# Four-layer gated cross-attention stack: where the FFN weights are loaded, and how the second attention opens

## The chip, the cores and the metric

One core of a Trainium2 chip runs the whole program in one launch. The metric is the device time of that core in microseconds (us). The engines are TensorE (PE, with its weight loads as PEld), VectorE (DVE), ScalarE (ACT), GpSimd (POOL) and SyncE (SP); SP issues nearly all transfers of this kernel, a few come from ACT's queue.

## The reference

Sixteen batches of 256 tokens with 256 features pass four residual layers. The context has 77 rows per batch.

```python
x = x + tanh(g_xattn[0]) * attention_16_heads_of_16(layernorm(x), ctx)     # q, k, v, out with biases
x = x + tanh(g_ffn[0])   * quantised_ffn(layernorm(x))                     # 768 hidden, 4-bit weights in blocks of 32
x = x + tanh(g_xattn[1]) * attention_8_heads_of_64(layernorm(x), ctx)
x = x + tanh(g_ffn[1])   * butterfly_ffn(layernorm(x))                     # W_exp, 10 stages, gelu, 10 stages, W_con

# attention:      softmax(q k^T / sqrt(d)) v, then the output projection
# quantised_ffn:  act_qdq around every product; weights wq = clip(round(w / s)) * s, s = max|w| / 7 per block
# butterfly:      per stage, pairs (i, i + 2^stage) are mixed by 2 x 2 matrices
```

## The kernel before

**Arithmetic.** Every fp32 product is done as three passes of rounded halves (`three_passes`, L41 to L43: hi x hi, hi x lo, lo x hi). x stays in SBUF as `xres` over the whole program. The butterfly stages are multiplied out on the chip to two matrices, w1 (tile `f_y`) and w2 (`f_z`), beside the quantised FFN; both are stored to DRAM (`w_spill`) and loaded back for the last layer.

**First attention** (`stacked_attention`). It runs in slots, one for each batch b, and each engine has its own written order of steps for a slot: `PE_SLOT`, `DVE_SLOT` and so on, SP's at L658. In a slot the engine works on several batches: the load of x (`xl`) and its layer norm (`ln`) are for batch b+4, the queries for b+3, the stacked keys and queries for b+2 (`qw`, `qr`, `k0`, `k1`), the maxima of the scores (`mx0` to `mx7`) for b+1, and the output with its update of x (`pu`) for b-1. SP's steps are `xl` (L149, x of b+4), `qw` (L327, stores the queries to DRAM), `vb` (L772), `k0` and `k1` (L318, keys), `qr` (L336 and L338, loads the queries back as a stack), and at b = 0 and b = 1 `save`: the values of the second attention are stored to DRAM (L287), since the tile that holds them, `a_keys_then_fw`, is to take the raw FFN weights. At b = 1 SP then waits until these stores are read (L292) and loads the three weight matrices (`load_ffn`, 768 KB each). A slot is called by its b below. Its DVE order begins with maxima `mx0` to `mx3`, then `ln`, then `mx4` to `mx7` and `pu` (L924). From slot 3 on (`FW_FIRST`) a few quantising steps `w0` to `w5` (L65 to L75) stand between them in each slot; they all wait for one semaphore that counts the three loads.

**The quantised FFN's last block and the passage.** The last block of `quantised_ffn` computes the down projection and, on the side, the last butterfly product, whose two additions POOL does (L2325). SP issues what the second attention needs first: weights `wq` and `wo`, the saved values (L2357), the first keys (L2365), a picking mask (L2368), and then the store of w1 (L2370). At its end SP waits for both stores (L2371, L2372), as they sit in tiles that the next block reuses. A block of the program ends with a barrier over all engines (L48, L49).

**Second attention** (`late_attention`). Again slots by batch, with the orders that `slots` takes. Its first slots are partial: slot -2 and -1 prepare batches 0 and 1. Batch 0's queries come from the block before, in banks `T0` and `X0`. Per batch: ACT rounds the queries to `q_hi` (L1354); DVE splits off the remainder (L1508); the upper halves are copied by DMA to two tiles (L1363 for batch 0, on ACT's queue; L1246 later); SP loads the keys `kb` (L1265) and `kz` (L1259); PE multiplies q_hi by `kz` into the bank `T0` in four groups and DVE reduces each to maxima (`mx0` to `mx3`, L1614 and L1515); PE transposes the maxima (`mt`, L1620), ACT spreads them over rows of `a_q_max` (L1374), and the scores (`s0` to `s3`, L1639 and L1641) take them as part of the contraction. `kb` also holds, in part 1 of its middle index, the picking mask, which ACT writes for the two first buffers (`pick`, L1319) before the keys may be loaded over its rows (L1265). POOL clears `a_q_max` (L1280) and `kz[1]` (L1281) at the start. At batch 0's `mt` ACT also computes the gate's tanh (L1368) and, one instruction later, the first exp (L1369), which brings in that function's table.

## Time and profile before

| | |
|---|---|
| Time, three runs | 1073.12 us median (1069.98, 1073.12, 1073.65) |
| The profiled execution | 1070.05 us, of it 1068.3 us span |
| PE, PEld busy | 927.3 us (87%), 821.2 us (77%) |
| DVE busy | 769.8 us (72%) |
| ACT, POOL busy | 604.2 us (57%), 283.2 us (27%) |
| Mean granted clock of PE | 0.938 of full |

Start times in the rows are us from the span's start. In a row of the timeline the bracket says how long the engine had been idle and what released it. "SPq" and "ACTq" are DMA issues on these engines' queues. Slot 1 of the first attention runs at about 76 to 88 us, slot 2 at 88 to 112, slot 3 at 113 to 125, and the passage into the second attention lies between 600 and 660 us. A granted clock of 1.00 is TensorE at 2.4 GHz, 0.50 is 1.2 GHz.

### The profile page before, as it was taken

To read this page: it belongs to the slowest core of one execution; us is meant where nothing else is said; L and a number is where in the kernel's file an instruction comes from. 1 tells how busy PE (TensorE), PEld (TensorE's weight loads), DVE (VectorE), ACT (ScalarE), POOL (GpSimd) and SP (SyncE) were. 2 spreads that over 40 slices of the span, in tenths; PEclk is the share of its full clock that TensorE was granted. 3 is DMA by queue.
4 is the path that set the end of the run, shared out by engine and by line. 5 is a ranking of instruction groups with operands and counts; after the bars stand their busy time and mean duration, and the time that the engine had idled before them with its cause. 6 is when DMAs were issued, how large, how long until landed. Compare 5 with 4: busy or idle time off the path is not lost. (4 is left out here: it accounts for less than half of the span.)

```text
span 1068.3 us, 19975 instructions
## 1 busy us (share of the span) xinstructions
PE 927.3 (87%) x6641; PEld 821.2 (77%) x6641; DVE 769.8 (72%) x1556; ACT 604.2 (57%) x1048; POOL 283.2 (27%) x480
## 2 busy tenths in 40 slices
PE   5896989999969999960369858999999979999998
PEld 5775877877767887750259857999999968988898
DVE  5534878887656888998987835777777869667671
ACT  4354666776646758879958625665666544222230
POOL 5302333330118914430014221111111123111210
PEclk9998999999988999985579987999999999999999
DMA  7657555565064317878801066655555510001001
GB/s 211 176 158 228 131 149 143 148 199 157 10 250 176 156 42 226 257 260 276 281 40 40 25 180 149 127 126 126 126 126 121 110 40 1 21 22 39 20 20 40
DMA packets 100137, 137.01 MB, mean 128 GB/s; under 512 B 42710, under 2 KB 75734, under 8 KB 97382
## 3 DMA queue, kind: packets, MB, share of 16 engines
q1 hardware_dynamic: 99158, 133.87, 44.2%
q10 hardware_dynamic: 608, 1.18, 0.4%
q0 software_dynamic: 304, 1.10, 0.3%
q8 instruction: 38, 0.62, 0.3%
q14 instruction: 29, 0.24, 0.1%
HBM read 68.47 MB, written 45.82 MB: 107 GB/s over the span
## 5 line engine op out<-in xcount | busy, mean ns | idle before, releaser
L2762 ACT ACTIVATE f_h<-bank,f_b 128x512 f32<-128x512 f32 x64 | 43.4, 690 | 112.3 <-PE bank L43 64.5
L912 DVE TENSOR_REDUCE a_maxima<-bank 128x4 f32<-128x308 f32 x128 | 60.4, 472 | 45.1 <-PE bank L1000 44.1
L41 PE MATMUL bank<-f_xt_hi,f_w_all 128*128 128x512 f32 x192 | 78.0, 406 | 6.8 <-DMA f_xt_lo<-x_spill 4.8
L835 ACT ACTIVATE a_prob<-bank 77x512 f32<-77x512 f32 x128 | 72.4, 588 | 18.5 <-PE bank L1025 18.2
L43 PE MATMUL bank<-f_xt_hi,f_w_all 128*128 128x512 f32 x192 | 76.6, 399 | 0.0
L42 PE MATMUL bank<-f_xt_lo,f_w_all 128*128 128x512 f32 x192 | 76.6, 399 | 0.0
L43 PE MATMUL bank<-f_w_hi,f_h_lo 128*128 128x256 f32 x256 | 72.4, 283 | 0.0
L42 PE MATMUL bank<-f_w_lo,f_h_hi 128*128 128x256 f32 x256 | 72.3, 282 | 0.0
L41 PE MATMUL bank<-f_w_hi,f_h_hi 128*128 128x256 f32 x256 | 72.0, 281 | 0.0
L1022 PE MATMUL bank<-a_stack,a_kb 96*77 96x256 f32 x256 | 70.9, 301 | 0.5 <-ACT a_mt L828 0.5
L1927 DVE TENSOR_REDUCE f_gmax<-f_hid 128x1 f32<-128x1024 f32 x48 | 55.6, 1213 | 15.4 <-ACT f_hid L2053 15.4
L1656 PE MATMUL bank<-a_values,a_prob 77*128 (+1 forms) x512 | 66.5, 273 | 0.0
L1025 PE MATMUL bank<-a_mt,a_pick 128*77 128x256 f32 x256 | 66.4, 283 | 0.0
L1000 PE MATMUL bank<-a_kb,a_stack 96*128 96x156 f32 x256 | 50.9, 281 | 17.6 <-DVE a_maxima L912 9.9
L1656 PEld LDWEIGHTS bank<-a_values,a_prob 77*128 77x128 f32 x512 | 62.2, 192 | 0.0
L41 PE MATMUL bank<-f_d_hi,f_w_all 128*128 128x256 f32 (+2 forms) x174 | 52.6, 302 | 7.6 <-DVE xres L2399 3.9
L1000 PEld LDWEIGHTS bank<-a_kb,a_stack 96*128 96x128 f32 x256 | 40.3, 194 | 23.4 <-DVE a_maxima L912 12.4
L41 PE MATMUL bank<-a_wo_hi,a_at_hi 128*128 128x256 f32 x192 | 57.6, 300 | 0.0
L43 PE MATMUL bank<-a_wo_hi,a_at_lo 128*128 128x256 f32 x192 | 54.4, 284 | 0.0
L42 PE MATMUL bank<-a_wo_lo,a_at_hi 128*128 128x256 f32 x192 | 54.4, 284 | 0.0
L1022 PEld LDWEIGHTS bank<-a_stack,a_kb 96*77 96x77 f32 x256 | 37.7, 147 | 21.1 <-issue 8.6
L41 PE MATMUL bank<-f_xt_hi,f_w_hi 128*128 128x512 f32 x128 | 51.8, 405 | 1.3 <-ACT f_h L2762 1.3
(332 smaller groups left out, 3181.2 us busy)
## 6 DMA issues: line engine op xcount, KB each, us to landing
u_spill<-f_ubuf SPq DMA_DIRECT2D x48, 256.0 KB, 2.4
f_w_all<-u_spill SPq DMA_DIRECT2D x24, 512.0 KB, 5.2
a_stack<-a_queries SPq DMA_DIRECT2D x16, 512.0 KB, 5.0
a_q_max<-a_q_hi SPq DMA_DIRECT2D x30, 256.0 KB, 4.5
a_kb<-a_key_spill SPq DMA_DIRECT2D x96, 77.0 KB, 2.6
xres<-in_x SPq DMA_DIRECT2D x16, 256.0 KB, 4.8
a_queries<-a_q_hi SPq DMA_DIRECT2D x16, 256.0 KB, 3.6
a_queries<-a_q_lo SPq DMA_DIRECT2D x16, 256.0 KB, 4.5
```

The costliest lines, as they stand in the source:

```text
L41: nc.tensor.matmul(out, w_hi, m_hi, start=start, stop=False)
L42: nc.tensor.matmul(out, w_hi, m_lo, start=False, stop=False)
L43: return nc.tensor.matmul(out, w_lo, m_hi, start=False, stop=stop)
L835: act.activation(prob[0:S, n % 4, :, :].rearrange("p a b -> p (a b)"), (S0, S1)[n % 2][0:S, :], ACT.Exp, scale=SCALE).then_inc(probs, 1)
L912: dve.tensor_reduce(maxima[:, t, 4 * k:4 * k + 4], MX[:, 0:4 * SE].rearrange("p (h s) -> p h s", s=SE)[:, :, 0:S], AX.X, ALU.max).then_inc ...
L1000: last = pe.matmul(MX[:, 2 * n * SE:2 * (n + 1) * SE], stack[0:ROWS, par, pair, t * P:(t + 1) * P], kb[0:ROWS, par, :, pair, :], start=Tru ...
L1022: pe.matmul(out, kb[0:ROWS, par, a, pair, 0:S], stack[0:ROWS, par, pair, :], start=True, stop=False)
L1025: last = pe.matmul(out, pick[:, 2 * pair + a, 0:S], mt[:, par, :], start=False, stop=True)
L1656: last = pe.matmul(out_of(t, h), prob[0:S, n % 2, a, t * P:(t + 1) * P], v, start=True, stop=True)
L1927: dve.tensor_reduce(gmax[:, side, m // 2:m // 2 + 1], hid[:, 2 * g:2 * g + 2, f - 1:f + 1, :], AX.XYZ, op).then_inc(g_maxed, 1)
L2762: act.activation(h[:, n % 2, :], hbank[n % 4][:, :], ACT.Gelu, bias=b1[:, n:n + 1]).then_inc(h_ready, 1)
```

## The change

There are two independent parts. In the first attention SP gets a step `fw` of its own at the end of slot 2 (b = `FW_FIRST - 1`), behind that slot's `k1`; the wait for the value stores and the loads of the FFN weights move there from the end of slot 1. The semaphore `fw_in` becomes three, one for each matrix (in `load_ffn` each load counts its own), and the quantising step of the first slot waits for the gate matrix alone; later ones wait for all three.

In the passage: the store of w1 stands behind the first keys' load, ahead of the mask and the values. DVE writes the picking mask (`pick0`, `pick1`) in an order `DVE_FIRST` that slot -1 alone uses, and there the four maxima come before the split of the queries. Batch 0's scores for the maxima go to four banks (S0, S1, O0, O1), need only the rounded queries, and its transposed maxima go to T1, so PE need not wait for DVE between groups. The keys of part 0 are loaded before part 1, and only part 1 waits for the mask. The gate's tanh and the exp that brings its table are done in the quantised FFN's blocks, the loads of the gate leave the passage and that of `bo` goes to SP behind batch 1's keys. POOL clears `a_q_max` for batch 0 only at the start and the rest after batch 1's layer norm, for which SP gets one more wait at batch 1.

```diff
@@ -655,7 +656,7 @@
-        SP_SLOT = "xl qw vb k0 qr k1 save keep".split()
+        SP_SLOT = "xl qw vb k0 qr k1 save fw keep".split()
@@ -663,7 +664,7 @@
-        ONLY_AT = {"save": (0, 1), "keep": (B - 6, B - 5, B - 4), "rk": (B - 3,), "sk": (B - 3,)}
+        ONLY_AT = {"save": (0, 1), "fw": (FW_FIRST - 1,), "keep": (B - 6, B - 5, B - 4), "rk": (B - 3,), "sk": (B - 3,)}
@@ -734,9 +735,9 @@
                         save_value(sp, i)
-                    if b == 1:
-                        sp.wait_ge(v1_saved, 16 * NV1)
-                        load_ffn(sp)
+                elif what == "fw":
+                    sp.wait_ge(v1_saved, 16 * NV1)
+                    load_ffn(sp)
@@ -901,7 +902,11 @@
                 elif what[0] == "w":
-                    dve.wait_ge(fw_in, 48)
+                    if isinstance(b, int) and b == FW_FIRST:
+                        dve.wait_ge(fw_in[0], 16)
+                    else:
+                        for loaded in fw_in:
+                            dve.wait_ge(loaded, 16)
@@ -1190,17 +1194,28 @@
+        DVE_FIRST = "pick0 ln mx0 mx1 mx2 mx3 q0 q1 pick1 xt".split()
...
-        def slots(eng, order, step, prepare=()):
+        def max_bank(b, g):
+            return (S0, S1, O0, O1)[g] if isinstance(b, int) and b == 0 else T0
+        def spread_bank(b):
+            return T1 if isinstance(b, int) and b == 0 else T0
+        def slots(eng, order, step, prepare=(), opening=None):
...
-                for what in order:
-                    if what in PRE:
+                for what in (opening or order) if isinstance(b, int) and b == -1 else order:
+                    if what[:4] == "pick":
+                        step(what, b, par)
+                    elif what in PRE:
@@ -1241,6 +1256,8 @@
                     sp.sem_inc(sp_passed, 1)
+                    if isinstance(b, int) and b == 1:
+                        sp.wait_ge(mt_cleared, 2 * HPC)
@@ -1258,12 +1275,16 @@
                                      late["k_dram"][own[a], 0, :, bass.ds(b * S, S)]).then_inc(kz_in[par], 16)
-                    if isinstance(b, int) and b < 2:
-                        sp.wait_ge(picked, b + 1)
-                    for a in range(HPC):
-                        for part, rows in ((0, own[a]), (0, across[a]), (1, own[a])):
-                            sp.dma_start(kb[rows, par, a, part, :, :].bitcast(F32),
-                                         late["k_dram"][own[a], part, :, bass.ds(b * S, S)]).then_inc(keys_in[par], 16)
+                    for part in range(2):
+                        if part and isinstance(b, int) and b < 2:
+                            sp.wait_ge(picked, b + 1)
+                        for a in range(HPC):
+                            for rows in (own[a], across[a])[0:2 - part]:
+                                sp.dma_start(kb[rows, par, a, part, :, :].bitcast(F32),
+                                             late["k_dram"][own[a], part, :, bass.ds(b * S, S)],
+                                             ).then_inc(keys_in[par], 16)
+                    if isinstance(b, int) and b == 1:
+                        sp.dma_start(bo_raw[:], gbias).then_inc(small_in, 16)
@@ -1276,12 +1297,11 @@
-            for a in range(HPC):
-                pool.memset(q_max[a][:].bitcast(F32), 0.0).then_inc(mt_cleared, 1)
-            pool.memset(kz[1][:].bitcast(F32), 0.0).then_inc(kb_cleared, 1)
...
+            def clear_max(par):
+                for a in range(HPC):
+                    pool.memset(q_max[a][:, par, :, :].bitcast(F32), 0.0).then_inc(mt_cleared, 1)
+            clear_max(0)
@@ -1297,6 +1317,12 @@
                     pool.tensor_tensor(nmr[:], nmean[:], rstd[:], ALU.mult).then_inc(ln_nmr, 1)
+                    if isinstance(b, int) and b == 1:
+                        pool.memset(kz[1][:].bitcast(F32), 0.0).then_inc(kb_cleared, 1)
+                        clear_max(1)
@@ -1315,16 +1341,9 @@
         def _(act):
-            def pick(n):
-                act.activation(kb[:, n, :, 1, :, :], late["pick_raw"][:, :, :, 0:S], ACT.Copy).then_inc(picked, 1)
...
                     if isinstance(b, int) and b == 0:
-                        act.dma_start(gate_raw[:], gate).then_inc(small_in, 16)
-                        act.dma_start(bo_raw[:], gbias).then_inc(small_in, 16)
-                        act.wait_ge(late["pick_in"], 16)
-                        pick(0)
@@ -1354,7 +1373,6 @@
-                        pick(1)
@@ -1363,16 +1381,14 @@
-                    if isinstance(b, int) and b == 0:
-                        act.wait_ge(small_in, 32)
-                        act.activation(tg[:], gate_raw[:], ACT.Tanh).then_inc(g_done, 1)
-                        act.activation(warm[:], gate_raw[:], ACT.Exp)
-                        act.wait_ge(mt_cleared, HPC)
+                    if isinstance(b, int) and b < 2:
+                        act.wait_ge(mt_cleared, (b + 1) * HPC)
...
-                                                  T0[0:HEADS, 0:T].unsqueeze(1).to_broadcast([HEADS, c1 - c0, T]),
+                                                  spread_bank(b)[0:HEADS, 0:T].unsqueeze(1).to_broadcast(
+                                                      [HEADS, c1 - c0, T]),
@@ -1437,6 +1453,10 @@
                     return
+                elif what[:4] == "pick":
+                    n = int(what[4])
+                    dve.wait_ge(late["pick_in"], 16)
+                    dve.tensor_copy(kb[:, n, :, 1, :, :], late["pick_raw"][:, :, :, 0:S]).then_inc(picked, 1)
@@ -1452,7 +1472,7 @@
-                        dve.wait_ge(g_done, 1)
+                        dve.wait_ge(small_in, 16)
@@ -1512,7 +1532,8 @@
-                    dve.tensor_reduce(maxima[:, t, h0:h0 + 4], T0[:, 0:4 * S].rearrange("p (h s) -> p h s", s=S),
+                    dve.tensor_reduce(maxima[:, t, h0:h0 + 4],
+                                      max_bank(b, g)[:, 0:4 * S].rearrange("p (h s) -> p h s", s=S),
@@ -1604,20 +1626,23 @@
-                        pe.wait_ge(q_split, b * NP + 1)
+                        if isinstance(b, int) and b == 0:
+                            pe.wait_ge(q_rounded, 1)
+                        else:
+                            pe.wait_ge(q_split, b * NP + 1)
...
-                    if not (isinstance(b, int) and b == 0 and g == 0):
+                    if not (isinstance(b, int) and b == 0):
...
-                        last = pe.matmul(T0[:, at:at + HPC * S], q_hi[:, n, t * P:(t + 1) * P],
+                        last = pe.matmul(max_bank(b, g)[:, at:at + HPC * S], q_hi[:, n, t * P:(t + 1) * P],
...
-                        last = pe.transpose(T0[0:HEADS, t * P:(t + 1) * P], maxima[:, t, :], ident[:])
+                        last = pe.transpose(spread_bank(b)[0:HEADS, t * P:(t + 1) * P], maxima[:, t, :], ident[:])
@@ -2231,6 +2257,7 @@
                 act.activation(tg[:], tg[:], ACT.Tanh)
+                act.activation(env["first"].tg[:], env["first"].tg[:], ACT.Tanh)
@@ -2351,12 +2378,6 @@
                 weight("wo")
-                wait_coded(sp, late["values_free"])
-                for half in range(2):
-                    bs = slice(half * B // 2, (half + 1) * B // 2)
-                    sp.dma_start(late["values"][0:S, bs, :, :].rearrange("p b h v -> p b (h v)"),
-                                 late["v_dram"][bs.start * S:bs.stop * S, :].rearrange("(b s) n -> s b n", s=S),
-                                 ).then_inc(late["values_in"][half], 16)
@@ -2364,10 +2385,16 @@
                                  late["k_dram"][half, 0, :, 0:S]).then_inc(first.kz_in[0], 16)
+                sp.wait_ge(y_add, 2 * TOP)
+                sp.dma_start(bf["w1_dram"], y[:]).then_inc(y_stored, 16)
...
                 sp.dma_start(late["pick_raw"], late["picks"]).then_inc(late["pick_in"], 16)
-                sp.wait_ge(y_add, 2 * TOP)
-                sp.dma_start(bf["w1_dram"], y[:]).then_inc(y_stored, 16)
+                wait_coded(sp, late["values_free"])
+                for half in range(2):
+                    bs = slice(half * B // 2, (half + 1) * B // 2)
+                    sp.dma_start(late["values"][0:S, bs, :, :].rearrange("p b h v -> p b (h v)"),
+                                 late["v_dram"][bs.start * S:bs.stop * S, :].rearrange("(b s) n -> s b n", s=S),
+                                 ).then_inc(late["values_in"][half], 16)
@@ -2497,6 +2524,7 @@
+                act.activation(warm[:], tg[:], ACT.Exp)
```

SP's order in the first attention around slots 1 to 3; `a_value_spill` is the value store, `a_keys_then_fw<-in_w_...` are the weights, `xres<-in_x` is x of b+4. Before:

```order
L287 DMA a_value_spill<-a_keys_then_fw 128x520 x4
L287 DMA a_value_spill<-a_raw 80x520
L292 DMA a_keys_then_fw<-in_w_gate 128x6x256
L292 DMA a_keys_then_fw<-in_w_up 128x6x256
L294 DMA a_keys_then_fw<-in_w_down 128x2x768
L149 DMA xres<-in_x 128x2x256
L327 DMA a_queries<-a_q_hi 128x512
L327 DMA a_queries<-a_q_lo 128x512
L772 DMA a_vb<-a_values 77x512
L318 DMA a_kb<-a_keys 16x624 x3
L336 DMA a_stack<-a_queries 64x2048
L338 DMA a_stack<-a_queries 32x2048
L318 DMA a_kb<-a_keys 16x624 x3
L149 DMA xres<-in_x 128x2x256
```

After:

```order
L288 DMA a_value_spill<-a_keys_then_fw 128x520 x4
L288 DMA a_value_spill<-a_raw 80x520
L149 DMA xres<-in_x 128x2x256
L328 DMA a_queries<-a_q_hi 128x512
L328 DMA a_queries<-a_q_lo 128x512
L773 DMA a_vb<-a_values 77x512
L319 DMA a_kb<-a_keys 16x624 x3
L337 DMA a_stack<-a_queries 64x2048
L339 DMA a_stack<-a_queries 32x2048
L319 DMA a_kb<-a_keys 16x624 x3
L293 DMA a_keys_then_fw<-in_w_gate 128x6x256
L293 DMA a_keys_then_fw<-in_w_up 128x6x256
L295 DMA a_keys_then_fw<-in_w_down 128x2x768
L149 DMA xres<-in_x 128x2x256
```

The three weight loads stood ahead of slot 2's x, queries, keys and stack; they now stand behind them and ahead of slot 3's x.

SP's order in the last block of the quantised FFN (`w_spill<-f_y` is the store of w1, `a_rest<-in_picks` the mask). Before:

```order
L2351 DMA w_spill<-f_z 128x2048
L2348 DMA a_raw<-in_wqkv 128x2x512
L2348 DMA a_raw<-in_wo 128x4x256
L2357 DMA a_values<-a_value_spill 77x8x520 x2
L2365 DMA a_kz<-a_key_spill 64x4x77 x2
L2368 DMA a_rest<-in_picks 128x624
L2370 DMA w_spill<-f_y 128x2056
```

After:

```order
L2378 DMA w_spill<-f_z 128x2048
L2375 DMA a_raw<-in_wqkv 128x2x512
L2375 DMA a_raw<-in_wo 128x4x256
L2386 DMA a_kz<-a_key_spill 64x4x77 x2
L2389 DMA w_spill<-f_y 128x2056
L2391 DMA a_rest<-in_picks 128x624
L2395 DMA a_values<-a_value_spill 77x8x520 x2
```

The store of w1 moved ahead of the mask and of the saved values.

DVE's order in the opening of the second attention, from the start of its block (`a_maxima<-bank` are the maxima, `f_xt_hi` and `f_xt_lo` the split of the queries, `a_kb<-a_rest` the mask). Before:

```order
L1444 BN_STATS a_bn<-xres 128x6 x2
L1452 BN_AGGR a_mv<-a_bn 128x2 x2
L1508 TENSOR_TENSOR f_xt_hi<-bank,a_q_hi 64x512
L1508 TENSOR_TENSOR f_xt_lo<-bank,a_q_hi 64x512
L1515 TENSOR_REDUCE a_maxima<-bank 128x4
L1508 TENSOR_TENSOR f_xt_hi<-bank,a_q_hi 64x512
L1508 TENSOR_TENSOR f_xt_lo<-bank,a_q_hi 64x512
L1515 TENSOR_REDUCE a_maxima<-bank 128x4 x3
L1499 TENSOR_TENSOR a_xt_lo<-bank,a_xt_hi 128x512
```

After:

```order
L1459 CAST a_kb<-a_rest 128x2x308
L1464 BN_STATS a_bn<-xres 128x6 x2
L1472 BN_AGGR a_mv<-a_bn 128x2 x2
L1535 TENSOR_REDUCE a_maxima<-bank 128x4 x4
L1528 TENSOR_TENSOR f_xt_hi<-bank,a_q_hi 64x512
L1528 TENSOR_TENSOR f_xt_lo<-bank,a_q_hi 64x512
L1528 TENSOR_TENSOR f_xt_hi<-bank,a_q_hi 64x512
L1528 TENSOR_TENSOR f_xt_lo<-bank,a_q_hi 64x512
L1459 CAST a_kb<-a_rest 128x2x308
L1519 TENSOR_TENSOR a_xt_lo<-bank,a_xt_hi 128x512
```

The four maxima stand together ahead of the split, and DVE has the two mask copies that were ACT's.

## Rows read from the trace of the kernel before

**Rows 1.** Timeline of SP's DMA issues: start, length, queue, line, transfer, count.

```profile
86.22 0.55 SPq L287 DMA_DIRECT2D a_value_spill<-a_raw  x1
92.41 0.38 SPq L292 DMA_DIRECT2D a_keys_then_fw<-in_w_gate  x1
...
94.01 0.75 SPq L149 DMA_DIRECT2D xres<-in_x  x1
...
103.61 0.49 SPq L336 DMA_DIRECT2D a_stack<-a_queries  x1
...
104.83 1.27 SPq L318 DMA_DIRECT2D a_kb<-a_keys  x3
```

**Rows 2.** Timeline of DVE, slots 2 and 3.

```profile
102.05 0.75 DVE L176 BATCH_NORM_STATS2 a_bn<-xres 128x6 f32<-128x256 f32 x2 [8.68 <-DMA xres<-in_x]
...
103.14 0.45 DVE L912 TENSOR_REDUCE a_maxima<-bank 128x4 f32<-128x308 f32 x1
...
110.70 0.88 DVE L924 SCALAR_TENSOR_TENSOR xres<-bank,a_tg,xres 128x256 f32<-128x256 f32 x2 [1.02 <-PE bank L43]
...
118.08 0.73 DVE L176 BATCH_NORM_STATS2 a_bn<-xres 128x6 f32<-128x256 f32 x2
...
119.16 0.45 DVE L912 TENSOR_REDUCE a_maxima<-bank 128x4 f32<-128x308 f32 x1
...
123.86 0.88 DVE L924 SCALAR_TENSOR_TENSOR xres<-bank,a_tg,xres 128x256 f32<-128x256 f32 x2 [0.17 <-PE bank L43]
```

**Rows 3.** Windows: length, busy us of PE, PEld, DVE, ACT, POOL, clock, DMA share, GB/s.

```profile
96.00:100.00 4.00, 0.00 (x0) 0.00 (x0) 0.00 (x0) 0.00 (x0) 0.00 (x0) 0.98 1.06 387
...
104.00:108.00 4.00, 4.00 (x24) 3.05 (x23) 2.15 (x4) 1.90 (x5) 0.61 (x2) 0.50 0.82 178
```

**Rows 4.** DMA issues, 85 to 125 us: count, KB each, median us to landing.

```profile
a_stack<-a_queries SPq DMA_DIRECT2D x2, 256.0 KB, 5.7
```

**Rows 5.** Waits of PE, 112 to 290 us: total, times, longest.

```profile
PE bank L1000 <- DVE a_maxima L912: 1.1, 2, 0.6
```

**Rows 6.** Waits of SP, 575 to 665 us: total, times, longest.

```profile
SPq L2372 <- DMA w_spill<-f_y: 11.4, 1, 11.4
```

**Rows 7.** Timeline of SP, 596 to 662 us.

```profile
615.96 3.60 SPq L2370 DMA_DIRECT2D w_spill<-f_y  x1
634.25 5.08 SPq L1265 DMA_DIRECT2D a_kb<-a_key_spill  x6
```

**Rows 8.** DMA issues, 596 to 650 us: KB, us to landing.

```profile
w_spill<-f_y SPq DMA_DIRECT2D x1, 1028.0 KB, 15.0
```

**Rows 9.** Timeline of POOL, same stretch.

```profile
597.97 5.06 POOL L2325 TENSOR_TENSOR f_y<-f_y,f_y_pair 128x1028 f32<-128x1028 f32 x2 [8.41 <-ACT f_y L2477]
...
632.59 3.54 POOL L1280 MEMSET a_q_max<- 128x2048 f32 x2 [17.69 <-POOLq L49]
```

**Rows 10.** Timeline of PE, same stretch.

```profile
627.27 0.28 PE L43 MATMUL bank<-a_rows_hi,a_wq_lo 128*128 128x256 f32 x1
636.28 0.68 PE L1614 MATMUL bank<-a_kz,a_q_hi 128*128 128x154 f32 x2 [8.73 <-DVE f_xt_lo L1508]
...
643.87 0.47 PE L1639 MATMUL bank<-f_xt_hi,a_kb 128*77 128x256 f32 x1 [0.41 <-DMA a_kb<-a_key_spill]
...
645.88 0.41 PE L1641 MATMUL bank<-a_q_max,a_kb 128*77 128x256 f32 x1
646.36 0.58 PE L41 MATMUL bank<-a_xt_hi,a_wq_hi 128*128 128x256 f32 x1
```

**Rows 11.** Timeline of ACT, same stretch.

```profile
635.23 0.53 ACTq L1363 DMA_DIRECT2D f_xt_hi<-a_q_hi  x1
...
639.66 1.28 ACT L1369 ACT_TABLE_LOAD   x1
...
642.72 2.39 ACT L1374 ACTIVATE a_q_max<-bank 8x256 fp32r<-8x256 f32 x4 [1.56 <-PE bank L1620]
```

**Rows 12.** Source line L2719, all its 64 casts: shortest, median, longest in ns.

```profile
L2719 DVE CAST f_h_hi<-f_h x64: 411/422/961, 881.3 to 1041.3; 128x512 fp32r<-128x512 f32 x64
```

**Rows 13.** Timeline of DVE and of POOL, 896 to 903 us.

```profile
898.74 0.96 DVE L2719 CAST f_h_hi<-f_h 128x512 fp32r<-128x512 f32 x1
...
897.54 3.90 POOL L2738 TENSOR_TENSOR xres<-xres,f_gb 128x256 f32 x4 [1.63 <-DVE f_xn L2709]
```

More of the change, by code:

```diff
@@ L220, in stacked_attention @@
         q_moved, kb_moved, vb_moved = ([sem(f"{x}{par}") for par in range(2)] for x in ("q_moved", "kb_moved", "vb_moved"))
-        sp_passed, scores, fw_in = sem("sp_passed"), sem("scores"), sem("fw_in")
+        sp_passed, scores = sem("sp_passed"), sem("scores")
+        fw_in = [sem(f"fw_in{n}") for n in range(3)]
         q_stored = [sem("q_stored0"), sem("q_stored1")]
@@ L1106, in late_tensors, with late_attention @@
     late["pick_raw"] = late["rest"][:, 0:heads * (S + S % 2)].rearrange("p (a c s) -> p a c s", c=C, s=S + S % 2)
-def late_attention(nc, env, gbias, gate):
+def late_attention(nc, env, gbias):
     HEADS, d = 8, 64
@@ L1155, in late_attention @@
         gb = sb("gb", [P, D])
-        tg = sb("tg", [P, 1])
+        tg = first.tg
         warm = sb("warm", [P, 1])
         bo_raw = sb("bo_raw", [P, D])
-        gate_raw = sb("gate_raw", [P, 1])
         xn = nxt.xn[:, 1, 0:TT, :]
@@ L1179, in late_attention @@
         passed, sp_passed, small_in = sem("passed"), sem("sp_passed"), sem("small_in")
-        next_cleared, mt_cleared, picked, g_done, gb_ready, biased = (sem(x) for x in (
-            "next_cleared", "mt_cleared", "picked", "g_done", "gb_ready", "biased"))
+        next_cleared, mt_cleared, picked, gb_ready, biased = (sem(x) for x in (
+            "next_cleared", "mt_cleared", "picked", "gb_ready", "biased"))
         q_rounded, q_split = sem("q_rounded"), sem("q_split")
@@ L1403, in step @@
                     act.activation(nxt.w2_hi[:], nxt.v, ACT.Copy).then_inc(nxt.v_rounded, 1)
-                    act.activation(warm[:], gate_raw[:], ACT.Gelu)
+                    act.activation(warm[:], tg[:], ACT.Gelu)
                 elif what in ("at0", "at1"):
@@ L1535, in _ @@
                    (B - 1, "q0"): "turn0", (B - 1, "q1"): "turn1", (B - 1, "mx1"): "next_xn1",
-                   (B - 1, "mx2"): "turn2", (B - 1, "at1"): "turn3", (B - 1, "mx3"): "next_x", (B, "norm"): "next_w2"})
+                   (B - 1, "mx2"): "turn2", (B - 1, "at1"): "turn3", (B - 1, "mx3"): "next_x", (B, "norm"): "next_w2"},
+                  DVE_FIRST)
         @block.tensor
@@ L2104, in _ @@
                 sp.dma_start(tg[:], gate).then_inc(g_in, 16)
+                sp.dma_start(env["first"].tg[:], late["gate"]).then_inc(g_in, 16)
                 sp.dma_start(paths, bf["low_paths"]).then_inc(paths_in, 16)
@@ L2570, in sem @@
             return self.sems[-1]
+        self.tg = sb("gate", [P, 1])
         self.minus_half, self.eps, self.zero = sb("minus_half", [P, TT]), sb("eps", [P, TT]), sb("zero", [P, TT])
@@ L2841, in build @@
         env["keys_dram"] = nc.dram_tensor("a0_keys", (2, B, P, DC, S + S % 2), F32, kind="Internal").ap()
-        env["late"] = late = {"ctx_t": a["ctx_t"], "wqkv": a["wqkv1"], "wo": a["wo1"], "picks": a["picks1"],
+        env["late"] = late = {"ctx_t": a["ctx_t"], "wqkv": a["wqkv1"], "wo": a["wo1"], "picks": a["picks1"], "gate": a["gx1"],
                               "inner": 512, "heads": 8}
@@ L2859, in build @@
                                   a["out_bias"], a["gf1"])
-            late_attention(nc, env, a["bo1"], a["gx1"])
+            late_attention(nc, env, a["bo1"])
             free_semaphores(nc, env["late"]["sems"] + env["first"].sems)
```

12 lines of the change are left out of this document (6 added, 6 removed).

## The prediction

> **What bounds the kernel now.** The page first: PE is busy 87% of the span, so a stretch in which PE stands still, or runs at the lower clock, is the place to look. The timeline of DVE shows the first one. In slot 2 DVE waits 8.68 us before the layer norm, and the releaser is the load of x [rows 2]. The maxima `mx4` to `mx7` stand behind that norm in DVE's order and PE has no free bank without them: from 96 to 100 us all engines are at zero while the DMA engines run at 387 GB/s, and afterwards PE works at clock 0.50 [rows 3]. SP's timeline says why x is late. The last value store is issued at 86.22, then SP waits until 92.41 for these stores, issues the three weight loads, and only at 94.01 the load of x [rows 1]. So x is issued some 7.2 us later than SP was free, and behind 2.3 MB.
>
> The second place is the passage. The wait list of SP has 11.4 us for the store of w1 at the block's end [rows 6]. That store is issued at 615.96 [rows 7] and lands 15.0 us later, at 630.96 [rows 8]; what it stores was ready at 597.97 + 5.06 = 603.03 [rows 9], and PE was done at 627.55 [rows 10]. The next block's first work starts at 632.59 [rows 9], 1.63 after the landing. I call this start T0. From there PE's first full stretch begins with the queries of batch 1 (`q0`) at 646.36, T0 + 13.77 [rows 10].
>
> **Part 1, the weight loads behind slot 2.** Removed: the 8.68 us. With SP free at 86.8, x for slot 2 is issued there and has only the value stores beside it; they are read by 92.4, when SP's wait for them ends [rows 1], and `ln` is reached at 102.05 - 8.68 = 93.4 [rows 2]. So x comes in time by about 1 us. Also removed: the slow clock behind the stall. From `mx4` to the update of x slot 2 needs 110.70 - 103.14 = 7.56 us, slot 3 the same work in 123.86 - 119.16 = 4.70 [rows 2]; 2.86 us more at the lower clock. Together 11.54.
>
> Given back in slot 3: its x now stands behind the weights. Slot 2's stack is issued at 103.61 before, when PE restarts, so now near 94.9; its `k1` follows and ends 2.49 us later [rows 1], at 97.4, and the weights follow. Slot 3's norm is reached at 118.08 before [rows 2], now at 106.5. When is x there? Lower bound: all that is issued from 94.9 on is 768 KB of stack, 117 KB of keys, 2304 KB of weights and 256 KB of x, 3.5 MB, at 387 GB/s [rows 3] 9.1 us, so 104.0: no wait. Upper bound: before, 102.05 - 92.41 = 9.64 us passed from the first weight load to x [rows 1, 2]; with the stack's own 5.7 us [rows 4] still wholly ahead, 97.4 + 9.64 + 5.7 = 112.7, a wait of 6.2. Without the stack's share it is 107.0, a wait of 0.5. The stack has half of its time behind it at 97.4, and the rate above is one with nothing small in it, so I take 107.7, a wait of **1.2** us. The first quantising step needs only the gate matrix now, the first of the three, so it doesn't add to this. The new waits for two more semaphores in each later step are on DVE, for which PE waits 1.1 us in twice from 112 to 290 us [rows 5]: nothing, at most 1. Part 1 gives 11.54 - 1.2 = **10.3** us (5.3 at the upper bound, and less if the clock falls again: 2.5).
>
> On this the Trainium skill (*DMA: Bandwidth & Descriptors*, section "Queues, rings and completion order") says that each DMA engine takes the descriptors of a queue's ring in ring order. The trace agrees: x issued at 94.01 came only at 102.05. By that rule x of slot 3 can't overtake the weights, and the saving is that of my sum as long as the weights are through before the norm; by it, the wait moves rather than goes if they aren't, the first rival below.
>
> **Part 2, the passage.** (a) The store of w1 is issued at about 603 to 606 now and, with 15.0 us at most, is down by 621, before PE ends at 627.55. What ends the block is then PE. With the same 1.63 us to the next block's first work the start is 629.2, T0' = T0 - **3.4**. The values and the mask stand behind the store; the values are not issued before 609.97 either way, since SP waited there for their tile, and PE needs them only in slot 0.
>
> (b) Within the passage two chains run to the first scores `s0`: the maxima and the DMAs. The chain of maxima is `mx0` at 636.28, T0 + 3.7, behind DVE's split [rows 10], four rounds of matmul and reduce, `mt`, and ACT's spreading at 642.72 to 645.11, T0 + 10.1 to 12.5 [rows 11]. In it go the three round trips, the split and the 1.28 us table load [rows 11]. With four banks the products follow ACT's rounding directly: from the rounding's end near T0' + 1.6, four pairs of 0.7 [rows 10], reduce and transposes about 1, the spreading 2.4 [rows 11], so done at about T0' + 8. The other chain: `s0` at 643.87 waited last for the keys [rows 10], first issued at 634.25 [rows 7], 9.62 us before. They were issued at T0 + 1.66, since ACT had to write the mask first; now part 0 is issued at T0' + 0.1. Then `s0` can start at T0' + 9.7 rather than T0 + 11.28, 1.6 us earlier. From `s0` to the end of `s1` are 646.29 - 643.87 = 2.4 us, in which 0.18 was a wait for ACT, so `q0` at T0' + 12.0 against T0 + 13.77 [rows 10]: **1.8** us. The DMA chain sets this, so the shorter maxima gain nothing beyond it. If the transfers land sooner, since 1.4 us less is queued and the upper halves are issued earlier than at 635.23 [rows 11], the maxima's chain allows `q0` at about T0' + 9 to 10, a gain of 4 to 5. If the keys land as late as before, it is 0.
>
> (c) The two mask copies on DVE: 128 x 616 each. The nearest row is the cast of 128x512, 422 ns in the median, but 961 at most [rows 12]; the long ones lie under an op of GpSimd [rows 13]. So 0.5 to 1.2 us each. In slot -1 DVE waits for ACT's rounding and for PE between its steps, and the chain that sets the end is the DMA's; nothing is charged. If that cover is gone, the first one puts 1 us in front of the norm.
>
> The Trainium skill (*SBUF — State Buffer*, section "SBUF: two separate sides") says that VectorE and GpSimd take a shared port pair as an exclusive lock for a whole instruction. It speaks against this edit, as POOL clears `a_q_max` in the same microseconds; the trace agrees with 961 against 422 ns. By the rule the first copy takes up to 1 us instead of 0.5, which the DMA chain still covers, so the sum stays.
>
> (d) tanh and the table load go to stretches where ACT is not waited for: nothing. POOL's second clearing, half of 3.54 us [rows 9], lies behind batch 1's norm, and SP needs it only for batch 1's copies, which follow `q0`: nothing.
>
> Part 2 gives 3.4 + 1.8 = **5.2** us (3.4 to 8.4).
>
> **Sum.** 10.3 + 5.2 = 15.5 us. Against the profiled execution, 1070.05, that is 1054.5; against the median of the three runs, 1073.12, it is 1057.6. I take the middle, **1056.0**.
>
> **Rivals.**
> *B, the wait moves to slot 3.* The weights delay x and the stack there by the upper bound: 6.2 us of wait, and the clock falls again for 2.9. For it: 2.3 MB in one queue ahead of x, as before. Against it: no 5.6 us wait of SP ahead of them, and the norm is reached 9 us after their issue. Gain 2.5 to 5.3 + 5.2 = 7.7 to 10.5: 1061.
> *C, better.* The transfers of the passage land sooner and the clock stays up there: 10.3 to 11.5 + 8.4: 1051.
> *D, the passage keeps only the block's earlier end.* 10.3 + 3.4, minus an exposed mask copy of 1: 1059.
> *E, slower.* Slots of the first attention lose their clock again and again, because PE meets small waits in each of the slots 3 to 12 beside the weights' arithmetic on DVE. A dip costs 2.86 us [rows 2]; eight of them are 22.9, against the 15.5 gained 7.4 slower: 1079. Against it: PE waits for DVE only twice from 112 to 290 us [rows 5]. It decides from the eighth dip on.
> *F, no change*: both stalls have something behind them that lasts as long. Nothing in the windows shows it.
>
> **Chances.** Main 0.62, B 0.17, C 0.10, D 0.06, E 0.02, F 0.03. The measurement tells about 0.5%, 5.4 us, from no change. Main, B, C and D lie beyond it but for a small part of B: faster 0.94, same 0.04, slower 0.02. The range takes in main with its bounds and C below (with the lower of the two bases, 1070.05, it gives 1050; with some spread 1049) and most of B above: 1049 to 1063.
>
> **What would show it.** In the profile after: the norm of slot 2 without its 8.7 us wait and clock 1.00 from 96 to 104; the weights issued behind slot 2's `k1` near 97 us; a wait of DVE for x in slot 3 of 0 to 2 us. SP's wait for the store of w1 gone and the block's end set by PE, 3 to 4 us earlier against PE's last matmul; `s0` about 9.7 us behind the new block's start, its releaser a DMA; DVE's mask copies between 0.5 and 1.2 us. The forecast is wrong if slot 3's wait is over 5 us, if PE's clock drops in slots 3 to 12, or if `s0` starts no sooner behind the block's start than 11 us.

## The result, and the profile after

The changed kernel takes 1060.98 us, the median of 15 runs (1057.24 to 1068.16), against 1072.7 us for the kernel before in 15 runs on the same chips; the ratio is 0.9903, 95% interval 0.9884 to 0.9922, so 8.4 to 12.4 us faster. One of the 15 runs before took 1361.8 us; the ratio goes by the fast runs alone. The median lies inside the range of 1049 to 1063 and 5.0 us above the 1056.0. The gain by the ratio, 10.4 us, is two thirds of the 15.5 of the forecast's sum. The profiled execution of the changed kernel took 1061.93 us, its span is 1060.2 us, mean granted clock 0.941.

The first place, slots 2 and 3. DVE's timeline after, against [rows 2]:

```profile
95.07 0.74 DVE L176 BATCH_NORM_STATS2 a_bn<-xres 128x6 f32<-128x256 f32 x2
...
100.86 0.88 DVE L929 SCALAR_TENSOR_TENSOR xres<-bank,a_tg,xres 128x256 f32<-128x256 f32 x2 [0.19 <-PE bank L43]
...
107.20 0.54 DVE L65 TENSOR_REDUCE a_fw_scale<-a_keys_then_fw 128x12 f32<-128x384 f32 x1
...
111.79 0.75 DVE L176 BATCH_NORM_STATS2 a_bn<-xres 128x6 f32<-128x256 f32 x2 [3.10 <-DMA xres<-in_x]
...
120.57 0.88 DVE L929 SCALAR_TENSOR_TENSOR xres<-bank,a_tg,xres 128x256 f32<-128x256 f32 x2 [1.14 <-PE bank L43]
```

Slot 2's norm has no wait any more. The wait for x has moved to slot 3: 3.10 us, where 8.68 stood in slot 2. SP's timeline says how x got there, against [rows 1]:

```profile
97.75 1.27 SPq L319 DMA_DIRECT2D a_kb<-a_keys  x3
99.07 0.42 SPq L293 DMA_DIRECT2D a_keys_then_fw<-in_w_gate  x1
...
100.71 1.51 SPq L149 DMA_DIRECT2D xres<-in_x  x1
```

The loads follow slot 2's `k1`, and x of slot 3 is issued at 100.71 and used at 111.79, 11.1 us later. The windows (length, busy us of PE, PEld, DVE, ACT, POOL, clock, DMA share, GB/s), against [rows 3]:

```profile
96.00:100.00 4.00, 4.00 (x40) 3.50 (x39) 3.39 (x9) 2.98 (x7) 1.23 (x4) 1.00 0.61 135
100.00:104.00 4.00, 3.89 (x35) 3.03 (x35) 2.56 (x9) 2.91 (x7) 2.21 (x5) 1.00 0.99 237
...
116.00:120.00 4.00, 4.00 (x23) 3.11 (x23) 2.50 (x6) 2.40 (x6) 1.41 (x2) 0.50 0.92 184
```

PE is busy at clock 1.00 where it stood still before, but behind the new wait it has 0.50 again. And from 96 to 104 us, while slot 2's stack and keys are loaded and the weights begin, the DMA engines move 135 and 237 GB/s, not 387; in the first of these windows they are busy for 0.61 of the time, in the second for 0.99.

The second place, the passage. Timelines after of SP, PE and DVE, and POOL's first work of the new block, against [rows 7, 9, 10]:

```profile
599.00 0.34 SPq L2389 DMA_DIRECT2D w_spill<-f_y  x1
...
623.30 0.28 PE L43 MATMUL bank<-a_rows_hi,a_wq_lo 128*128 128x256 f32 x1
...
624.98 1.84 POOL L1302 MEMSET a_q_max<- 128x1024 f32 x2 [14.04 <-POOLq L49]
...
625.11 2.04 DVE L1459 CAST a_kb<-a_rest 128x616 fp32r<-128x616 f32 x1 [3.48 <-PEq L49]
...
632.98 0.48 DVE L1459 CAST a_kb<-a_rest 128x616 fp32r<-128x616 f32 x1
...
635.34 0.47 PE L1664 MATMUL bank<-f_xt_hi,a_kb 128*77 128x256 f32 x1 [1.16 <-DMA a_kb<-a_key_spill]
...
637.10 0.41 PE L41 MATMUL bank<-a_xt_hi,a_wq_hi 128*128 128x256 f32 x1
```

PE ends at 623.58 and the next block's first work comes at 624.98: 1.40 us, where there were 5.04 [rows 9, 10]. The store is issued when POOL's additions are done, and lands in 3.9 us, not 15.0 [rows 8]:

```profile
w_spill<-f_y SPq DMA_DIRECT2D x1, 1028.0 KB, 3.9
```

`s0` starts 10.36 us behind the block's start (11.28 before), and `q0` of batch 1 12.12 (13.77 before). The first mask copy on DVE takes 2.04 us, the second 0.48.

**The books of the two profiled spans**, 1068.3 and 1060.2: at POOL's additions (597.97 [rows 9], 593.91 after) the changed kernel is 4.1 us ahead, at the new block's start 7.6, at `q0` of batch 1 9.3, at the last rounding of queries in the second attention 10.9 (843.17 and 832.27), and at the last cast of the last layer 8.1 (1041.34 and 1033.22). So the passage gave 5.2 us, the second attention 1.6 more, all that lies ahead of POOL's additions 4.1 instead of the 10.3 forecast, and 2.8 were lost behind the second attention's last rounding, most of it in the opening of the last layer, which the change doesn't touch. Of the 4.1, slots 2 and 3 gave 3.6; slot 6 added 2.3 (16.79 to 14.46 us), which the change doesn't aim at: in the kernel before PE waits 1.93 us for keys there and its clock falls, in the changed kernel it doesn't. The rest was lost again in small steps.

### The profile page after: what moved, and what is told of

The parts are those of the page before. It is cut to its first block and busy times, and to the rows that moved or that the text cites. A ratio compares the mean times of both kernels' runs of the same rounds, so it can differ in the third digit from the quotient of the medians.

```text
span 1060.2 us, 20043 instructions
## 1 busy us (share of the span) xinstructions
PE 925.9 (87%) x6641; PEld 820.4 (77%) x6641; DVE 773.4 (73%) x1558; ACT 603.3 (57%) x1046; POOL 285.0 (27%) x482
## 5 line engine op out<-in xcount | busy, mean ns | idle before, releaser
L1952 DVE TENSOR_REDUCE f_gmax<-f_hid 128x1 f32<-128x1024 f32 x48 | 55.7, 1213 | 15.5 <-ACT f_hid L2078 15.5
```

Source lines behind the costliest of these rows:

```text
L1952: dve.tensor_reduce(gmax[:, side, m // 2:m // 2 + 1], hid[:, 2 * g:2 * g + 2, f - 1:f + 1, :], AX.XYZ, op).then_inc(g_maxed, 1)
```

## Experiments

All are edits of the changed kernel, but for the first. Medians are of 4 to 12 runs, ratios are to the kernel before on the same chip. In the profiles I read stretches, since the total holds clock dips from elsewhere; effects of 1 to 3 us between two variants of the changed kernel are not resolved by medians of so few runs (the store last, one bank and the keys behind the mask come to 1061.95, 1062.05 and 1062.31 us, the changed kernel to 1060.98). The length of a slot is taken between DVE's updates of x (L924 before, L929 after), in us:

| kernel | slot 2 | slot 3 | slot 4 | slot 5 | slot 6 |
|---|---|---|---|---|---|
| before | 24.69 | 13.16 | 13.71 | 14.30 | 16.79 |
| after | 14.58 | 19.71 | 13.17 | 14.99 | 14.46 |
| weights only | 13.15 | 19.00 | 13.20 | 14.28 | 14.02 |
| passage only | 25.71 | 13.47 | 21.14 | 13.97 | 14.76 |
| split loads | 13.41 | 13.68 | 13.91 | 14.78 | 14.34 |
| x first | 13.67 | 13.68 | 19.78 | 14.99 | 14.61 |
| keys first | 14.16 | 14.65 | 14.75 | 16.41 | 14.31 |
| split again | 13.48 | 13.70 | 13.86 | 14.68 | 14.74 |
| after again | 13.38 | 20.38 | 13.96 | 14.44 | 14.37 |

**1. Part 1 alone.** The kernel before with these lines (and with `fw` in `ONLY_AT` and the three semaphores, as in the change):

```diff
-        SP_SLOT = "xl qw vb k0 qr k1 save keep".split()
+        SP_SLOT = "xl qw vb k0 qr k1 save fw keep".split()
...
+                elif what == "fw":
+                    sp.wait_ge(v1_saved, 16 * NV1)
+                    load_ffn(sp)
```

> The kernel before with part 1 alone (weight loads at the end of slot 2, three semaphores). Part 1 as the profile after shows it: slot 2 gains 10.1 us, slot 3 gives 6.5 back (3.1 wait for x, about 2.9 for the lower clock, 0.5 else), 4.0 us are left at the end of the first attention. If the two parts add up, this is 4 us faster than before, about 1068.5 against a before of 1072.7. The rival (they don't add up: the stall of slot 3 depends on nothing in part 2, but the clock in later passages may move with time) would give anything from 1 to 8 us.

Measured: 1065.13 us, ratio 0.9961 (0.9938 to 0.9984), 4.2 us faster as expected. Slots 2 and 3 take 32.15 us together, 5.7 less than before.

**2. Part 2 alone.**

```diff
-        ONLY_AT = {"save": (0, 1), "fw": (FW_FIRST - 1,), "keep": ...
+        ONLY_AT = {"save": (0, 1), "fw": (FW_FIRST - 2,), "keep": ...
```

> The kernel after with the weight loads back at the end of slot 1, so part 2 alone. By the profile after: 3.55 us at the block's end, 1.65 to the queries of batch 1, and 1.6 that come in small steps over the second attention; 6.8 at the end of the second attention. The last layer's opening lost 2.8 us in the profile after, at a lower granted clock. If that loss belongs to part 2, this is only 4 us faster than before (1068.7); if it is chance or belongs to part 1, it is 6 to 7 faster (1066).

Measured: 1069.31 us, ratio 0.9984 (0.9966 to 1.0003): less than expected. Its profile has the passage's gains whole (1.40 us to the block's start, `q0` at 12.57), and the loss in slot 4, 21.14 us instead of 13.7. PE's timeline and the windows there:

```profile
130.21 0.71 PE L1005 MATMUL bank<-a_kb,a_stack 96*128 96x156 f32 x2 [1.66 <-DMA a_kb<-a_keys]
```

```profile
132.00:136.00 4.00, 4.00 (x23) 3.86 (x26) 1.63 (x7) 1.86 (x4) 0.00 (x0) 0.50 0.14 30
136.00:140.00 4.00, 4.00 (x26) 2.25 (x21) 2.64 (x9) 1.95 (x4) 0.03 (x1) 0.50 0.01 2
```

A wait of 1.66 us for the keys is followed by some 12 us at half clock. Nothing of part 2 lies near this slot; waits for these keys of up to 1.9 us are in the kernel before too, and from 112 to 290 us the clock falls after one of them only, of 1.93 us in slot 6. The two parts together were timed 10.4 us faster, the parts alone 4.2 and 1.7, so 4.5 us are missing from the sum. The half-widths of the three intervals, 2.0, 2.5 and 2.0 us, make about 3.8 together (root of the sum of squares), so the gap is a little wider than the noise. That such dips are what is missing is a guess; no run shows it. Of the opening of the last layer this run says that the loss isn't part 2's: from the last rounding of queries to the first cast of the last layer it takes 37.92 us, before 38.10, after 40.34, and part 1 alone 40.46.

**3. The weights split over three slots.**

```diff
-        ONLY_AT = {"save": (0, 1), "fw": (FW_FIRST - 1,), "keep": ...
+        ONLY_AT = {"save": (0, 1), "fw": (FW_FIRST - 1, FW_FIRST, B - 6), "keep": ...
...
-                    load_ffn(sp)
+                    load_ffn(sp, {FW_FIRST - 1: 0, FW_FIRST: 1, B - 6: 2}[b])
```

DVE's quantising steps wait for the first two matrices in slots 4 to 10 and for all three from slot 11 on.

> The kernel after, with one weight matrix at the end of slot 2 (the gate's), the second at the end of slot 3, the third at the end of slot 10. Theory L, x of slot 3 waits behind the volume of the weights: one third of the volume lets x land 4 us or so earlier, the 3.1 us wait is gone and the clock stays at 1.00, so 6.0 to 6.5 us faster than after, about 1054.7. Theory G, the loads cost by their volume wherever they lie: the wait comes back in two or three small pieces in later slots, at most 3 us faster, 1058 to 1061.

Measured: 1055.97 us, ratio 0.9878 (0.9843 to 0.9913). Slot 3 takes 13.68 us instead of 19.71 and has no wait for x. DVE's timeline:

```profile
93.95 0.74 DVE L176 BATCH_NORM_STATS2 a_bn<-xres 128x6 f32<-128x256 f32 x2
107.63 0.74 DVE L176 BATCH_NORM_STATS2 a_bn<-xres 128x6 f32<-128x256 f32 x2
```

The theory of the volume ahead of x holds, and the volume costs nothing in the later slots: none of slots 2 to 14 takes over 15 us in this profile or in that of the run that repeats it, and the clock falls in none.

**4. x of slot 3 ahead of the three loads.**

```diff
                 elif what == "fw":
+                    sp.wait_ge(x_loaded[1], 3 * 16)
+                    load(sp, 7, 1)
                     sp.wait_ge(v1_saved, 16 * NV1)
                     load_ffn(sp)
...
-                        if b < 2:
+                        if b < 2 or b == 7:
```

> The kernel after, with slot 3's x issued in slot 2 right ahead of the three weight loads. Theory L (order in the queue): x is there in time, no wait of DVE for x in slot 3, clock 1.00, 6 us faster than after, 1055. Theory G: queries, keys and stack of slot 3 still stand behind 2.3 MB, and one of them becomes the wait of 2 to 4 us in that slot or the next; 0 to 3 us faster, 1058 to 1061.

Measured: 1064.41 us, ratio 0.9938 (0.9908 to 0.9968). Slot 3 is clean, 13.68 us, and slot 4 takes 19.78. PE's timeline:

```profile
122.23 0.71 PE L1007 MATMUL bank<-a_kb,a_stack 96*128 96x156 f32 x2 [3.77 <-DMA a_kb<-a_keys]
```

So theory G was right for this edit: what stands behind the 2.3 MB is late, first x, and if x isn't, what follows; of the queries, stack and keys that follow, the row names the keys. It is the volume in one piece, not x's place, that costs 6 us.

**5. The store of w1 last again.** The values' block and the store go back to their places of before.

```diff
                 weight("wo")
+                wait_coded(sp, late["values_free"])
+                for half in range(2):
...
-                sp.wait_ge(y_add, 2 * TOP)
-                sp.dma_start(bf["w1_dram"], y[:]).then_inc(y_stored, 16)
                 wait_coded(sp, B)
                 sp.dma_start(late["pick_raw"], late["picks"]).then_inc(late["pick_in"], 16)
+                sp.wait_ge(y_add, 2 * TOP)
+                sp.dma_start(bf["w1_dram"], y[:]).then_inc(y_stored, 16)
```

> The kernel after, with the store of w1 back behind the values, the first keys and the mask. Read it in the profile, from the end of PE's last matmul of the block to the first work of the next one: 627.55 to 632.59 before (5.04 us), 623.58 to 624.98 after (1.40). The theory that the store's landing set the block's end and its place in the queue set the landing: back to 4.5 to 5.5 us. The rival that something else moved the end (the loads of the gate's and bo's rows, the table load): it stays below 2.5. In time 3.6 slower than after, about 1064, within the spread of the clock.

Measured: 1061.95 us, ratio 0.9928 (0.9901 to 0.9956). In the profile PE's last matmul ends at 622.73 and the new block's first work is at 628.40: 5.67 us, and SP's waits have the store back:

```profile
SPq L2399 <- DMA w_spill<-f_y: 11.8, 1, 11.8
```

This is shown: the store's place in the queue set the block's end. The 5.67 us lie a little over the 4.5 to 5.5 expected.

**6. One bank for the four groups of batch 0.** `max_bank` gives S0 for all four, and PE waits for the reduce of the group before.

> The kernel after, with batch 0's four groups of scores for the maxima in one bank, so that PE waits for DVE's reduce between them as before. By the prediction's step (b) the scores s0 are set by the DMAs, so the longer chain of maxima (about 3 us more: three round trips of 1.2 each, less what lies under the mask copy) costs at most 1 us: from the block's start to q0 of batch 1 12.1 us after, 12 to 13 here. The rival, that the maxima's chain sets it (after, ACT's spreading ends at T0' + 8.6, only 1.7 before s0): 13.5 to 15.

Measured: 1062.05 us, ratio 0.9929 (0.9901 to 0.9958). From the block's start to `s0` 11.60 us, to `q0` 13.45, between the two expectations: 1.3 us later than after. `s0` has no wait of its own now; the transposes of `xn` ahead of it wait for DVE's split, which stands behind the maxima in this order and is late with them:

```profile
634.02 1.09 PE L1572 MATMUL bank<-ident,f_xn 128*128 128x128 f32 x4 [2.34 <-DVE f_xt_lo L1528]
```

So with one bank the chain of maxima and split sets the end, and the four banks are worth 1.3 us against the profile after, and 0.6 to 1.3 against the eight profiles of the next experiment.

**7. Batch 0's keys behind the mask.**

```diff
-                        if part and isinstance(b, int) and b < 2:
+                        if not part and isinstance(b, int) and b < 2:
```

> The kernel after, with all of batch 0's keys behind the mask again (the wait stands ahead of part 0 and not of part 1). The mask copy takes until 2.2 us behind the block's start. If the keys' loads set s0, as predicted, the keys are issued 2.2 us later and s0 and q0 of batch 1 come 1.5 to 2.2 us later (13.6 to 14.3 from the block's start, 12.1 after). The rival, that the copies of the upper halves on ACT's queue or the volume set it: less than 0.7 later.

Measured: 1062.31 us, ratio 0.9929 (0.9902 to 0.9957). The keys are issued 1.31 us behind the block's start rather than at once, and `s0` starts at 10.66, `q0` at 12.42. In the eight profiles with this opening untouched (after, passage only, the split twice, x first, store last, keys first, after again) `s0` is at 10.36 to 11.10 us. So the time at which the keys' loads begin to be issued doesn't set `s0`: step (b) of the prediction falls, though its number was near. Nor does the end of their issue: in these nine profiles `s0` comes 3.9 to 5.6 us behind the last of the six.

**8. Split, and the keys ahead of the stack in each slot.** `SP_SLOT` is "xl qw vb k0 k1 qr save fw keep".

> The kernel with the weight loads split over slots 2, 3 and 10, and in every slot the second half of the keys (k1, 117 KB) ahead of the stack (768 KB) in SP's order. Theory K: PE's small waits for the keys, 8.4 us in 12 times in the run with the split, come from the keys' place behind the stack; moved ahead, less than 3 us of waits are left and no clock dip in slots 3 to 12 can start from them, so 3 to 6 us faster than the split alone (1050 to 1053). The rival: both are needed at the same moment and the last of them lands when it did; the wait is then for the stack, the time that of the split, 1056 within 3.

Measured: 1066.82 us, ratio 0.9971 (0.995 to 0.9992), 10 us slower than the split alone by the two ratios: a miss. The waits of PE in the first attention's slots, with the count and the longest:

```profile
PE bank L1009 <- DMA a_stack<-a_queries: 8.2, 6, 1.6
PE bank L1009 <- issue: 7.8, 7, 1.6
```

The waits, 16.0 us, are about twice the 8.4 us of the split. Half of them end with the stack; for the other half the profile names no releaser. Behind two of them, of 1.57 and 1.65 us, the clock falls, and slots 5 and 7 take 16.41 and 16.49 us.

**9. Batch 1's keys held back.** In step `kb` of batch 1 SP first waits until the six loads of batch 0 have landed.

> The kernel after, with batch 1's keys and zero-padded keys issued only when batch 0's keys have landed. With the keys issued 1.3 us later, s0 came only 0.3 later, so their issue doesn't set it. Theory V (volume): the six key loads and the four copies of the upper halves share the DMA engines, and batch 1's loads, which are issued before the last of batch 0's lands, take a share too; held back, s0 comes 0.5 to 1.2 us sooner than the 10.36 us behind the block's start that the profile after shows. The rival, that the last load's own latency sets it: within 0.3. The loads of batch 1 end some 3 us later, and are needed about 5 us behind s0, so that little of it shows in the time.

Measured: 1067.09 us, ratio 0.9956 (0.9923 to 0.9989). `s0` starts at 10.05, 0.3 us sooner than in any of the eight profiles above; the volume theory wanted 0.5 to 1.2, so at most a small part is theirs. What was not expected is the price: batch 1's keys are issued at 638.7, PE waits 3.0 us before batch 1's maxima, where it waited 0.32 in the profile after, and has half clock from 648 to 664 us. The row names no releaser; that the late keys are what it waited for is argued from the edit.

```profile
648.77 0.68 PE L1640 MATMUL bank<-a_kz,a_q_hi 128*128 128x154 f32 x2 [3.04 <-issue]
```

**10. POOL clears the maxima tiles only behind the first mask.**

```diff
+            pool.wait_ge(picked, 1)
             clear_max(0)
```

> The kernel after, with POOL's clearing of the maxima tiles started only when DVE has written the first mask. The first mask copy took 2.04 us in the profile after, 1.15 in two others, and the second one, of the same shape, 0.48. The theory of the shared port: alone, the first takes 0.5 too, the norm and the maxima behind it come up to 1.5 us sooner, and s0 stays within 0.4 of 10.36, since DMAs set it (the two copies that wait for the clearing are issued about as before). The rival, that a first instruction behind a barrier or the mask's fresh landing makes it long: it stays above 1 us.

Measured: 1060.76 us, ratio 0.9877 (0.9822 to 0.9933). Timelines of DVE and POOL:

```profile
623.96 0.48 DVE L1460 CAST a_kb<-a_rest 128x616 fp32r<-128x616 f32 x1 [3.48 <-PEq L49]
...
624.50 1.84 POOL L1302 MEMSET a_q_max<- 128x1024 f32 x2 [14.72 <-DVE a_kb L1460]
```

The copy takes 0.48 us once POOL isn't clearing beside it, where it took 2.04 or 1.15, though it still is DVE's first instruction behind the barrier. `s0` comes 10.8 us behind SP's first issue of the block, no sooner, 0.4 later than after. The expectation holds. This profile has another slot 3, too: PE waits 1.66 us for the keys at its start and has half clock for some 3 us, then DVE waits only 0.70 for x, and the slot takes 17.33 us. In the seven other profiles with the weights loaded whole at slot 2's end and x behind them it takes 19.0 to 20.4 us, with 2.4 to 3.6 of waiting for x.

**11 and 12. The split and the kernel after once more, side by side.**

> The kernel with the weight loads split over slots 2, 3 and 10 once more, beside the kernel after on the same chip. By the two profiles it is 6.0 us faster in slots 2 and 3. If the medians follow, the ratio is near 0.985 here and 0.990 for the kernel after; if slots further on give it back by dips of the clock, both are near 0.989.

> The kernel after once more, as the base for the split. Slot 3 again at 19 to 20.5 us with a wait of 2 to 3.5 us for x, slot 2 at 13.2 to 14.6; about 1061.

Measured: split 1057.33 us, ratio 0.9848 (0.9808 to 0.9888); after 1061.59 us, ratio 0.9886 (0.9844 to 0.9928). Slot 3 repeats to 0.7 us, slot 2 to 1.2 (table). The split is 4 to 5 us faster than the kernel after in both pairs of medians (1055.97 and 1057.33 against 1060.98 and 1061.59); each single ratio's interval overlaps the other's. The split is shown to be faster than the kernel before; against the changed kernel the two pairs and the repeated 6 us in slot 3 agree, though the intervals don't part them.

## Why the prediction was right, and where it was off

The time fell inside the range, since the range had been drawn to take in most of rival B, and the forecast of both mechanisms held: the stall of slot 2 went, and so did the wait for the store. But the sum, 15.5 us, was half as much again as the 10.4 measured, above all by its term for slot 3; and one of the signs that the forecast named for being wrong did come: PE's clock dropped in slot 3. That the total came out so near to B's 1061 is partly luck: 2.3 us from a wait with a clock dip in slot 6, which the kernel before had in its profile and the changed one had not, and 1.6 in the second attention, stand against 2.8 lost behind it, and none of the three was forecast.

**The stall of slot 2.** Right. Slot 2 lost its 8.68 us wait and the low clock behind it: 24.69 to 14.58 us, and 13.2 to 13.7 in most other kernels with this order, so 10.1 to 11.5 against the 11.54 forecast.

**What comes back in slot 3.** This is the term that was mis-sized: "I take 107.7, a wait of 1.2 us". The measured wait is 3.10 us, and the slot took 19.71 us against 13.16, 6.5 us more, since the clock fell again. x was there at 111.8 us, not at 107.7, and the norm was reached at 108.7, not at 106.5, which hid half of this. Three things made it. The rate of 387 GB/s came from a stretch with the weights' loads above all; with the stack's and keys' loads in it the engines moved 135 and 237 GB/s. SP issued the weights at 99.07, 1.7 us later than the 97.4 of the sum. And the price of the clock, 2.86 us, which I had taken from the trace, I charged only in the lower bound and in rival B; in all profiles where PE stopped for 2.3 to 3.8 us in slots 3 and 4 it was to pay. Rival B put a total gain of 7.7 to 10.5 us and 1061 on this, with a chance of 0.17, and it is the kind of thing that happened, with a wait half as long as B's 6.2: part 1 gave 3.6 us in slots 2 and 3 of the profile, 4.2 timed alone. The likeliest case should have been B. The trace had the sign for it, the stack's own 5.7 us to land [rows 4].

The Trainium skill (*DMA: Bandwidth & Descriptors*, "Queues, rings and completion order") says that each DMA engine takes the descriptors of a ring in ring order. This told more than I took from it, and the runs agree: x behind the weights (a wait of 3.10 us), and in the run with x first the keys behind them (3.77 us), both came late.

**The block's end.** Right in mechanism and size: 3.64 us by the profile (5.04 to 1.40), 3.4 forecast, and the run with the store last has it back.

**From the block's start to batch 1's queries.** The forecast was 12.0 us, measured 12.12; 1.65 us gained, 1.8 forecast. The step was wrong all the same: it let `s0` start 1.6 us sooner because the keys are issued sooner, at 9.7; it started at 10.36, 0.9 sooner, and it hardly moves with the keys' issue (experiment 7). The rest, 0.7, came behind it: from `s0` to `q0` 1.76 us instead of 2.49. Before, PE's instructions there, which start 0.2 to 0.3 us apart otherwise, stood 0.59 apart where PE waited for ACT and 0.48 apart ahead of `q0`; after, there are no such gaps. Only the first of the two has a releaser in the trace. What sets `s0` is a landing of the keys, by its row; whether it is the copies on ACT's queue beside them stays open, since holding back batch 1's loads gave only 0.3.

**The mask on DVE.** The price was over the forecast's upper end: 2.04 us against "0.5 to 1.2", as the copy lay beside POOL's two clearing instructions. It was covered, as forecast. The Trainium skill (*SBUF — State Buffer*, "SBUF: two separate sides") says that of a GpSimd op and a VectorE op in a 2-port mode the one that starts first holds the shared port pair for its whole instruction. Experiment 10 agrees, with 0.48 us without POOL's clearing; that the copy runs in such a mode no run shows.

**Rival E**, dips in later slots, I had at eight dips to decide, and held against it only that PE waits for DVE twice. The same list of the kernel before has eight waits for the keys, 7.2 us in all, behind one of which, 1.93 us in slot 6, the clock falls. And one dip, in slot 4 of the run with part 2 alone, cost 7.4 us with its wait of 1.66, not 2.86: how long the clock stays down isn't the same each time.

**The last layer's opening.** It takes 1.4 to 2.5 us more in all profiles with the weights, or the first of them, loaded at slot 2's end, part 1 alone among them, and not in the two that load them at slot 1's. The work is the same and the last two waits of PE ahead of it are (0.68 and 0.48 us in both); the clock differs, 0.50 from 852 to 856 us in the profile after, and 1.00 in that of before at the same place in the work. Why is open; the forecast put nothing on it.

## What to carry to other kernels

When a large transfer is moved out of one slot's way, ask which small transfers stand behind it in its new place, and count them with the rates of what is in the queue with them; splitting 2.3 MB into three pieces, each ahead of its first use, gained what moving it in one piece gave back. A wait that stops TensorE can cost its length and the clock behind it, so price a moved wait from the length of its slot and not from the wait alone. Here waits of 2.3 to 3.8 us made a slot 5.3 to 6.7 us longer than the 13.7 of a clean one; 8.5 us of standing still cost 2.9 more; of the waits between 1.5 and 2 us some came with a fall of the clock and a slot 2.7 to 7.4 us longer, others without one and 1.3 us longer. A store that a block's end waits for belongs ahead of all loads that nobody waits for yet.

## What was not expected of the hardware

- The clock fell after waits as short as 1.57 us (keys first) and 1.66 us (part 2 alone) and in the second case stayed at half for 12 us of work; waits of 1.67 us (after) and 1.68 us (x first) were followed by nothing. So the length of the wait alone doesn't decide it; what does, no run here shows.
- The same store of 1028 KB lands 3.9 us after its issue with nothing queued ahead of it, and 15.0 us behind 3.0 MB of loads (the values, the first keys, the mask).
- A DVE copy of 128 x 616 takes 0.48 us alone, and 1.15 or 2.04 us beside POOL's clearing (two instructions of 0.95 us each), by the run. In the three profiles with 2.04 both clearing instructions keep their 0.95 us, so the copy ends 0.3 us behind the second; in the eight with 1.15 it ends 0.3 us behind the first, and the second takes 1.29 us. So each can hold up the other; what decides the order, no run shows.
